# One small attention stage of a fused Perceiver block: GpSimd's order of work, the query products' place, and the engines that mask queries and add the residual

## The chip, the cores and the metric

The kernel runs on one core of a Trainium2 chip. The metric is the device time of one execution in microseconds (us), lower is better. TensorE (PE) multiplies matrices, VectorE (DVE), ScalarE (ACT) and GpSimd (POOL) do the elementwise work, SyncE (SP) issues DMAs.

## What is computed

The reference passes 64 sequences of 32 tokens with 256 features through six residual blocks in turn. The change is in the fifth, a causal attention of 16 heads of 16 features, with four groups of keys and values:

```
x = x + attn1(layernorm(x))

q  = einsum('bse,hed->bhsd', x, Wq) + bq[None, :, None, :]
kg = einsum('bse,ged->bgsd', x, Wk) + bk[None, :, None, :]
vg = einsum('bse,ged->bgsd', x, Wv) + bv[None, :, None, :]
k, v = repeat(kg, 4, axis=1), repeat(vg, 4, axis=1)
scores = where(causal, -inf, einsum('bhqd,bhkd->bhqk', q, k) / sqrt(16))
out = einsum('bhqk,bhkd->bhqd', softmax(scores), v)
```

After it comes the sixth block, a mixture of eight experts (`silu(x @ gate) * (x @ up)` times `down`, one expert a token), whose weights are 8 x 512 KB each for gate, up and down.

## The kernel before

The 2048 tokens are 16 tiles of 128 rows (`TILES`), and `x_sb` keeps all of them on chip. Each residual block is a stage of its own (`nc.Block`): every engine has its own list of instructions, semaphores order them between engines, and all engines meet at the end of a stage.

`small_attention` is used twice: with `cross=True` for the first block, with `cross=False` for the fifth, which this text calls the last small attention. Its names in the profile begin with `attn_` and lie between 939 and 1054 us. It is a software pipeline over the tiles. In step i an engine does its part for several tiles at once: in TensorE's list these are the scores of tile i (`scores`, product `ps_scores`), the transposes of the exponentials of tile i-1 (`turn_exps`, `ps_pT`), keys and values of tile i+1 (`keys_values`, `ps_kv`), its queries (`queries`, `ps_q`), the transposes of the normalised rows of tile i+2 (`turn`, `ps_T`), and the weighing of the values of tile i-1 (`weigh`, `ps_o`). The full steps run in a loop unrolled by two (`run_steps`).

For a tile the work passes through the engines so:

- GpSimd normalises the rows into `xn`, one buffer for all tiles, so that tile t waits for the transposes of tile t-1 (`turned`).
- TensorE transposes `xn`, ScalarE copies it to `xnT`, TensorE makes keys, values and queries.
- ScalarE adds the key bias (`kT`). VectorE adds the value bias (`v_rows`), and SyncE moves the values through DRAM into `v_blocks` (one DMA out, four DMAs in).
- VectorE adds the query bias and masks the queries once for each of four heads of a group, one instruction for each half of the features (`q_blocks`, L468).
- TensorE's scores begin with two products (L320) that write the causal mask into `ps_scores`, and wait for queries and keys before them.
- VectorE turns the scores (L506), takes the maximum (L511), subtracts it (L514); ScalarE takes the exponential; TensorE and ScalarE turn it; TensorE weighs the values; VectorE divides (L482, L486 into `outs`), adds to `x_sb` (L496), and takes the row's statistics for the next stage (L110).

Four things stand at the stage's ends. GpSimd first blanks `v_blocks` and `v_rows` (L259, L260), then issues 16 DMAs for the experts' up and down weights (L2187), and then begins to normalise. VectorE takes the last tile's mean and root (`moments.roots`, 12 links from L117 to L180) in step -1. At the end VectorE takes the roots of the other 15 tiles for the next stage before it divides tile 15. TensorE starts with one product that nobody reads (`keep_busy`, L278).

The order in time on VectorE is that of `step`: divide and residual of tile i-2, scores of tile i, values and queries of tile i+1.

## Time and profile before

| | |
|---|---|
| median of 3 runs | 1257.46 us (1254.38 to 1261.32) |
| the profiled execution | 1256.03 us |
| its span in the profile | 1254.2 us |
| busy over the span | PE 1141.8, DVE 720.3, ACT 443.3, POOL 267.3 us |
| last small attention | about 939 to 1054 us of the span |
| experts' first product | 1111.23 us in the chain of waits |

The span reaches from the first to the last instruction that the profile shows, and the 1.8 us between it and the execution's time lie around it. Times of instructions are counted from the start of the span. A row with x8 is eight like instructions together, and the number before the engine is the time from the first start to the last end.

### The profile page before, as it was taken

The page shows a single profiled execution, that of the slowest core. Times are in us where ns is not written, and L with a number is a line of the kernel's source. Part 1 is how long each engine was busy: PE and PEld are TensorE (multiplying, and loading weights), DVE is VectorE, ACT ScalarE, POOL GpSimd, SP SyncE. Part 2 cuts the span into 40 slices and gives each one's busy share as a digit, 9 for nine tenths or more (in the row PEclk, how much of TensorE's full clock was granted, in tenths as well). Part 3 has the DMA queues.
Part 4 walks back from the last instruction along what each step waited for, and adds up shares of the span by engine and source line. Part 5 has one row for each costly group of instructions (what it writes and reads, how often), then busy time and mean ns, then how long its engine had stood idle before and what let it go on. Part 6 is the DMA issues. An engine that isn't in the chain of part 4 may idle for free. (4 is left out here: it accounts for less than half of the span.)

```text
span 1254.2 us, 32458 instructions
## 1 busy us (share of the span) xinstructions
PE 1141.8 (91%) x12589; PEld 872.6 (70%) x12590; DVE 720.3 (57%) x1834; ACT 443.3 (35%) x1283; POOL 267.3 (21%) x343
## 2 busy tenths in 40 slices
PE   3899899999999889999969999999984887889997
PEld 1676688787887668987957777777754775546664
DVE  3788554455455465553257878888763998212221
ACT  0444353443343211211046555555521332112221
POOL 1600000000000000000144456445415220322222
PEclk9999899999999989999689999999996997899999
DMA  7521000000000076000002111111148112122221
GB/s 234 180 58 45 1 1 1 0 0 0 0 0 1 1 197 156 0 0 9 27 10 54 48 32 51 51 42 35 44 153 277 37 32 80 40 60 38 43 39 14
DMA packets 69644, 65.54 MB, mean 52 GB/s; under 512 B 32720, under 2 KB 60656, under 8 KB 68940
## 3 DMA queue, kind: packets, MB, share of 16 engines
q1 hardware_dynamic: 61612, 45.32, 14.0%
q0 software_dynamic: 7968, 19.32, 5.2%
q8 instruction: 45, 0.74, 0.2%
q14 instruction: 19, 0.16, 0.0%
HBM read 52.34 MB, written 13.19 MB: 52 GB/s over the span
## 5 line engine op out<-in xcount | busy, mean ns | idle before, releaser
L1532 ACT ACTIVATE xattn_exps<-xattn_ps_s,xattn_top 128x256 f32<-128x256 f32 x256 | 118.0, 475 | 77.5 <-DVE xattn_top L1600 77.5
L613 PEld LDWEIGHTS attn_ps_q<-attn_xnT,w_b_q 128*128 128x128 f32 x1024 | 118.8, 193 | 12.6 <-issue 12.6
L613 PE MATMUL attn_ps_q<-attn_xnT,w_b_q 128*128 128x128 f32 x1024 | 123.4, 276 | 0.0
L1099 POOL TENSOR_TENSOR fold_last_cos<-raw_last,all_consts 64x64 f32<-64x64 f32 x1 | 0.3, 314 | 538.3 <-POOLq L911 538.3
L667 PE MATMUL attn_ps_out<-w_b_o,attn_oT 128*128 128x256 f32 x480 | 106.5, 380 | 1.8 <-DVE all_x L848 1.5
L667 PEld LDWEIGHTS attn_ps_out<-w_b_o,attn_oT 128*128 128x128 f32 x480 | 90.0, 190 | 15.1 <-DVE all_x L848 2.4
L1607 DVE STREAM_TRANSPOSE xattn_expsT<-xattn_exps 128x1024 f32<-128x1024 f32 x64 | 79.5, 1242 | 22.6 <-ACT xattn_exps L1532 22.6
L721 ACT COPY attn_qT<-attn_ps_q 128x512 f32<-128x512 f32 x64 | 38.0, 594 | 148.2 <-PE attn_ps_q L613 148.2
L1597 DVE TENSOR_REDUCE xattn_raw_top<-xattn_ps_s 128x4 f32<-128x1024 f32 x64 | 77.8, 1216 | 13.6 <-PE xattn_ps_s L1424 13.3
L1424 PE MATMUL xattn_ps_s<-xattn_kT,xattn_qT 64*32 64x256 f32 x2048 | 69.6, 381 | 2.9 <-ACT xattn_exps L1532 2.9
L1434 PE MATMUL xattn_ps_o<-xattn_expsT,xattn_kv 32*64 32x256 f32 x2048 | 63.5, 380 | 4.6 <-DVE xattn_last_scores L1643 3.9
L799 DVE BATCH_NORM_STATS2 attn_out_stats<-attn_ps_out 128x6 f32<-128x256 f32 x15 | 6.5, 432 | 103.2 <-PE attn_ps_out L667 103.2
L1399 PEld LDWEIGHTS xattn_ps_o<-xattn_xnT,all_d_a 128*128 128x128 f32 x512 | 61.4, 197 | 6.2 <-issue 6.2
L1399 PE MATMUL xattn_ps_o<-xattn_xnT,all_d_a 128*128 128x128 f32 x512 | 65.5, 283 | 0.0
L942 PE MATMUL ffn_ps_h<-ffn_xnT,all_c 128*128 128x128 f32 x512 | 62.4, 281 | 0.0
L959 PE MATMUL ffn_ps_out<-all_c,ffn_masked 128*128 128x256 f32 x256 | 59.7, 380 | 1.6 <-DVE ffn_masked L1041 1.6
L1462 PE MATMUL xattn_ps_o<-all_d_b,xattn_ctxT 128*128 128x256 f32 x240 | 55.4, 384 | 6.1 <-POOL xattn_ctxT L1350 4.5
L1434 PEld LDWEIGHTS xattn_ps_o<-xattn_expsT,xattn_kv 32*64 32x64 f32 x2048 | 44.3, 131 | 23.4 <-issue 11.2
L942 PEld LDWEIGHTS ffn_ps_h<-ffn_xnT,all_c 128*128 128x128 f32 x512 | 59.8, 196 | 0.0
L1894 POOL DMA_INDIRECT out<-experts_y_out,experts_about x23 | 35.9, 1559 | 110.2 <-ACT experts_y_out L1966 108.5
L1976 DVE COPY experts_hT<-experts_ps_h 128x512 f32<-128x512 f32 x23 | 15.9, 692 | 68.4 <-PE experts_ps_h L1923 68.4
L1462 PEld LDWEIGHTS xattn_ps_o<-all_d_b,xattn_ctxT 128*128 128x128 f32 x240 | 44.4, 190 | 13.9 <-issue 6.2
(325 smaller groups left out, 2309.2 us busy)
## 6 DMA issues: line engine op xcount, KB each, us to landing
xattn_inverse<-xattn_inverse_rows SPq DMA_DIRECT2D x30, 256.0 KB, 4.1
all_c<-in_ctx SPq DMA_DIRECT2D x64, 64.0 KB, 1.9
moe_gate<-in_f_gate SPq DMA_DIRECT2D x8, 512.0 KB, 8.6
moe_up<-in_f_up POOLq DMA_DIRECT2D x8, 512.0 KB, 7.2
moe_down<-in_f_down POOLq DMA_DIRECT2D x8, 512.0 KB, 12.9
sorted_x<-all_zeros SPq DMA_DIRECT2D x1, 2944.0 KB, 15.7
experts_x_in<-sorted_x SPq DMA_DIRECT2D x23, 128.0 KB, 2.3
xattn_v_stage<-xattn_v_rows SPq DMA_DIRECT2D x16, 136.0 KB, 1.8
```

Of the source, the lines that this page charges most:

```text
L613: last = nc.tensor.matmul(ps_q[g % 2][:, h * P:(h + 1) * P], wq[:, c, head * DH:(head + 1) * DH], xnT[u][:, c, :], start=(c == 0), stop=(c ...
L667: last = nc.tensor.matmul(bank[:, 0:DIM], of_heads[:, h, :, :].rearrange("p b q -> p (b q)"), wo[:, h, :], start=(h == 0), stop=(h == HEAD ...
L721: nc.scalar.copy(qT[:, :, g, :].rearrange("p b (h q) -> p h b q", h=PER), ps_q[g % 2][:, :].rearrange("p (h b q) -> p h b q", h=PER, b=TB) ...
L942: last = nc.tensor.matmul(ps_h[half][:, j * P:(j + 1) * P], w1[:, c, f * P:(f + 1) * P], xnT[:, c, :], start=(c == 0), stop=(c == KC - 1))
L959: last = nc.tensor.matmul(ps_out[:, 0:DIM], masked[u][:, f, :], w2[:, f, :], start=(f == 0), stop=(f == chunks - 1))
L1399: last = nc.tensor.matmul(ps_q[part][:, n * P:(n + 1) * P], a_w[:, c, m * P:(m + 1) * P], xnT[:, c, :], start=(c == 0), stop=(c == KC - 1))
L1424: last = nc.tensor.matmul(ps_s[g % 2][SEQ * b:SEQ * b + SEQ, 512 * odd + nkeys * n:512 * odd + nkeys * (n + 1)], qT[u][rows, b, 2 * g + n, :],
L1434: nc.tensor.matmul(ps_o[b][64 * odd:64 * odd + 64, 0:DIM], kv[u][rows, j, :], expsT[u][rows, :, odd, :, j, :], start=(j == 0), stop=False, ...
L1462: last = nc.tensor.matmul(out_bank(t), ctxT[:, m, :, :].rearrange("p b s -> p (b s)"), b_w[:, m, :], start=(m == 0), stop=(m == pairs - 1))
L1532: nc.scalar.activation(exps[g % 2][:, nkeys * k:nkeys * (k + 1)], ps_s[g % 2][:, nkeys * k:nkeys * (k + 1)], ACT.Exp, bias=top[u][:, n:n + ...
L1597: nc.vector.tensor_reduce(of_group(raw_top), ps_s[g % 2][:, :].rearrange("p (o m n) -> p o m n", o=2, m=2), X_AXIS, ALU.max, negate=True). ...
L1607: nc.vector.transpose(expsT[u][:, g, :, :, :, :].rearrange("p o m j q -> p (o m j q)"), exps[g % 2][:, :])\
```

## The change

In the last small attention (`cross=False`):

- GpSimd normalises tile 0 before it blanks the buffers. Then it normalises tiles 1 to 15, with one of the 16 weight DMAs issued after each, and, from tile 5 on, the residual addition of the tile five before (`POOL_LEAD`) after that. The last five additions and the last DMA follow.
- TensorE makes the queries right after the scores, before the transposes of the exponentials. Their second half goes to a free part of `ps_T`'s bank, so that `turn` waits for ScalarE to have read it (`q1_ready`).
- VectorE masks the first half of the queries alone, and now ahead of the values. ScalarE masks the second half with four activations (scale is the mask, bias a table `q1_bias` that VectorE makes once, after the last tile's roots). ScalarE waits for this table before its first copy.
- VectorE no longer adds the residual. It waits for GpSimd's addition before it takes the statistics, and these now stand at the end of its step.
- VectorE takes the last tile's roots at the start of the stage.

In both uses of `small_attention` the first causal-mask product no longer waits for queries and keys. The core of the diff:

```diff
+POOL_LEAD = 5
...
+    ps_qm = [ps_q[:, 0:P], ps_q[:, P:2 * P]] if cross else [ps_q[:, 0:P], ps_T[:, DIM:DIM + P]]
...
         @block.gpsimd
         def _(pool):
+            def normalise(t):
+                if t == TILES - 1:
+                    pool.wait_ge(dve_roots, Moments.LAST_LINKS)
+                wait_count(pool, turned, t)
+                nc.gpsimd.tensor_scalar(xn[:, :], x_sb[:, t, :], moments.moments[:, t, 0:1], moments.factors[:, t:t + 1],
+                                        ALU.subtract, ALU.mult).then_inc(xn_ready, 1)
+
+            if not cross:
+                normalise(0)
             for u in range(2):
                 nc.gpsimd.memset(v_blocks[u][:, :, :, :, :], 0.0).then_inc(blank, 1)
                 nc.gpsimd.memset(v_rows[u][:, :, :, HD], 1.0).then_inc(blank, 1)
-            if beside:
+            if cross:
                 beside(pool)
...
+            else:
+                loads = beside(pool)
+                for t in range(1, TILES + POOL_LEAD):
+                    if t < TILES:
+                        normalise(t)
+                        next(loads)
+                    if t >= POOL_LEAD:
+                        pool.wait_ge(o_ready, t - POOL_LEAD + 1)
+                        nc.gpsimd.tensor_tensor(x_sb[:, t - POOL_LEAD, :], x_sb[:, t - POOL_LEAD, :],
+                                                outs[:, :, :].rearrange("p h d -> p (h d)"), ALU.add).then_inc(x_ready, 1)
+                next(loads)
...
             def turn(t):
                 pe.wait_ge(xn_ready, t + 1)
+                if not cross:
+                    wait_count(pe, q1_ready, t)
...
             def scores(t):
-                pe.wait_ge(q_ready, t + 1)
-                pe.wait_ge(k_ready, t + 1)
                 wait_count(pe, scores_out, t)
                 for p in range(2):
+                    if p == 1:
+                        pe.wait_ge(q_ready, t + 1)
+                        if not cross:
+                            pe.wait_ge(q1_ready, t + 1)
+                        pe.wait_ge(k_ready, t + 1)
                     nc.tensor.matmul(ps_scores[:, 512 * p:512 * p + 256], ident16, causal16, start=True, stop=False, skip_group_check=True)
...
                 if live(0):
                     scores(i)
+                if not cross and live(1):
+                    queries(i + 1, 1 - u)
...
+            if not cross:
+                act.wait_ge(bias_made, 1)
+
+            def queries_out(t):
+                act.wait_ge(q1_made, t + 1)
+                for r in range(PER):
+                    last = nc.scalar.activation(q_blocks[:, 1, r, :], ps_qm[1], ACT.Identity, bias=q1_bias[:, r:r + 1],
+                                                scale=consts[:, C_QMASK + r:C_QMASK + r + 1])
+                last.then_inc(q1_ready, 1)
...
+                moments.roots(dve, dve_roots, EPS_LN, 1.0, LAST, x_sb)
                 for s, n in loaded:
                     dve.wait_ge(s, n)
+                nc.vector.tensor_scalar(q1_bias[:, :], consts[:, C_QMASK:C_QMASK + PER], w["bq"][:, 1:2], None, ALU.mult).then_inc(bias_made, 1)
...
                 if live(-2):
                     outs_ready(i - 2)
-                    if not cross:
-                        residual(i - 2)
...
                 if live(1):
+                    queries_out(i + 1)
                     if not cross:
                         values_out(i + 1, 1 - u)
-                    queries_out(i + 1)
-                if live(-2) and cross:
+                if live(-2):
                     residual(i - 2)
```

GpSimd, the whole beginning of the last small attention, before. `moe_up` and `moe_down` are the experts' weights, `attn_xn` the normalised rows.

```order
L259 MEMSET attn_v_blocks 128x1088
L260 MEMSET attn_v_rows 128x4
L259 MEMSET attn_v_blocks 128x1088
L260 MEMSET attn_v_rows 128x4
L2187 DMA moe_up<-in_f_up 128x2x512 x8
L2187 DMA moe_down<-in_f_down 128x4x256 x8
L268 TENSOR_SCALAR attn_xn<-all_x,all_moments,all_moments_work 128x256 x16
```

GpSimd now: the start of the stage, and after "..." the part of one full step (tiles 6 and 1), where the addition into `all_x` stands third.

```order
L266 TENSOR_SCALAR attn_xn<-all_x,all_moments,all_moments_work 128x256
L272 MEMSET attn_v_blocks 128x1088
L273 MEMSET attn_v_rows 128x4
L272 MEMSET attn_v_blocks 128x1088
L273 MEMSET attn_v_rows 128x4
L266 TENSOR_SCALAR attn_xn<-all_x,all_moments,all_moments_work 128x256
L2224 DMA moe_up<-in_f_up 128x2x512
...
L266 TENSOR_SCALAR attn_xn<-all_x,all_moments,all_moments_work 128x256
L2224 DMA moe_up<-in_f_up 128x2x512
L284 TENSOR_TENSOR all_x<-all_x,attn_outs 128x256
```

Tile 0's normalising has moved from behind 16 DMAs and four memsets to the front, and a full step holds three instructions where it held one.

VectorE, one step of the loop of full steps, before.

```order
L482 RECIPROCAL attn_inverse<-attn_ps_o 128x16
L486 TENSOR_TENSOR attn_outs<-attn_ps_o,attn_inverse 128x256
L496 TENSOR_TENSOR all_x<-all_x,attn_outs 128x256
L109 MEMSET all_carrier 128x1
L110 BN_STATS all_row_stats<-all_x 128x6
L506 STREAM_TRANSPOSE attn_scores<-attn_ps_scores 128x256 x2
L511 TENSOR_REDUCE attn_top<-attn_scores 128x16
L514 TENSOR_TENSOR attn_shifted<-attn_scores,attn_top 128x512
L476 TENSOR_TENSOR attn_v_rows<-attn_ps_kv,all_e_bv 128x4x16
L468 SCALAR_TENSOR_TENSOR attn_q_blocks<-attn_ps_q,all_e_bq,all_consts 128x512 x2
```

VectorE, the same step now.

```order
L523 RECIPROCAL attn_inverse<-attn_ps_o 128x16
L526 TENSOR_TENSOR attn_outs<-attn_ps_o,attn_inverse 128x256
L542 STREAM_TRANSPOSE attn_scores<-attn_ps_scores 128x256 x2
L547 TENSOR_REDUCE attn_top<-attn_scores 128x16
L550 TENSOR_TENSOR attn_shifted<-attn_scores,attn_top 128x512
L509 SCALAR_TENSOR_TENSOR attn_q_blocks<-attn_ps_q,all_e_bq,all_consts 128x512
L517 TENSOR_TENSOR attn_v_rows<-attn_ps_kv,all_e_bv 128x4x16
L110 MEMSET all_carrier 128x1
L111 BN_STATS all_row_stats<-all_x 128x6
```

The addition is gone, one of two query instructions is gone, and the statistics of tile i-2 (L111, which reads what GpSimd adds) stand last, right ahead of the next step's reciprocal.

TensorE, one step of the loop, now. Its second half of the queries is written to `attn_ps_T`.

```order
L346 MATMUL attn_ps_scores<-all_causal,all_ident 128x256
L352 MATMUL attn_ps_scores<-attn_q_blocks,attn_kT 32x128 x16
L332 MATMUL attn_ps_q<-attn_xnT,all_e_q 128x128 x2
L332 MATMUL attn_ps_T<-attn_xnT,all_e_q 128x128 x2
L361 MATMUL attn_ps_pT<-all_consts,attn_exps 128x128 x4
L321 MATMUL attn_ps_kv<-attn_xnT,all_e_k 128x128 x4
L324 MATMUL attn_ps_kv<-all_e_v,attn_xnT 128x64 x2
L306 MATMUL attn_ps_T<-all_consts,attn_xn 128x128 x2
L372 MATMUL attn_ps_o<-attn_v_blocks,attn_expsT 32x68 x16
```

Before, the four query products (L311) stood between the values and the transposes of `attn_xn`; the number of products is the same.

## Rows read from the trace of the kernel before

**Rows 1.** The page, busy time of the engines.

```profile
PE 1141.8 (91%) x12589; PEld 872.6 (70%) x12590; DVE 720.3 (57%) x1834; ACT 443.3 (35%) x1283; POOL 267.3 (21%) x343
```

**Rows 2.** Timeline, start of the stage: start us, us, engine, line.

```profile
939.15 1.00 POOL L259 MEMSET attn_v_blocks<- 128x1088 f32 x1 [16.35 <-POOLq L1301]
941.11 5.80 POOL L2187 DMA_DIRECT2D moe_up<-in_f_up  x8
952.92 1.24 POOL L268 TENSOR_SCALAR attn_xn<-all_x,all_moments,all_moments_work 128x256 f32<-128x256 f32 x1
954.30 0.66 PE L287 MATMUL attn_ps_T<-all_consts,attn_xn 128*128 128x128 f32 x2 [14.02 <-POOL attn_xn L268]
```

**Rows 3.** Busy by stretch: PE, PEld, DVE, ACT, POOL, then PEclk, DMA share, GB/s.

```profile
939.00:954.00 15.00, 1.10 (x2) 0.30 (x2) 0.00 (x0) 0.20 (x1) 14.80 (x21) 0.70 0.75 265
954.00:960.00 6.00, 5.17 (x23) 4.80 (x24) 0.23 (x1) 1.00 (x3) 1.37 (x2) 0.50 1.03 355
985.00:1040.00 55.00, 47.82 (x951) 40.22 (x932) 51.61 (x124) 21.59 (x51) 11.01 (x9) 1.00 0.17 33
```

**Rows 4.** Timeline of VectorE: the last tile's roots, and what follows.

```profile
961.49 0.42 DVE L117 BATCH_NORM_STATS2 all_row_stats<-all_x 128x6 f32<-128x256 f32 x1
964.32 0.78 DVE L506 STREAM_TRANSPOSE attn_scores<-attn_ps_scores 128x256 f32<-128x256 f32 x2
```

**Rows 5.** Timeline of TensorE: the score products of tiles 2 and 15.

```profile
973.85 0.67 PE L326 MATMUL attn_ps_scores<-attn_q_blocks,attn_kT 64*32 64x128 f32 x32
1043.47 0.67 PE L326 MATMUL attn_ps_scores<-attn_q_blocks,attn_kT 64*32 64x128 f32 x32
```

**Rows 6.** Timeline of VectorE, one full step.

```profile
985.91 0.76 DVE L506 STREAM_TRANSPOSE attn_scores<-attn_ps_scores 128x256 f32<-128x256 f32 x2
988.04 0.22 DVE L476 TENSOR_TENSOR attn_v_rows<-attn_ps_kv,all_e_bv 128x64 f32<-128x64 f32 x1
988.17 1.40 DVE L468 SCALAR_TENSOR_TENSOR attn_q_blocks<-attn_ps_q,all_e_bq,all_consts 128x512 f32<-128x512 f32 x2
989.49 0.25 DVE L482 RECIPROCAL attn_inverse<-attn_ps_o 128x16 f32<-128x16 f32 x1
989.77 0.42 DVE L486 TENSOR_TENSOR attn_outs<-attn_ps_o,attn_inverse 128x256 f32<-128x256 f32 x1
990.34 0.42 DVE L496 TENSOR_TENSOR all_x<-all_x,attn_outs 128x256 f32 x1
990.91 0.43 DVE L110 BATCH_NORM_STATS2 all_row_stats<-all_x  x1
```

**Rows 7.** Timeline of the same step: TensorE and GpSimd.

```profile
989.63 0.39 PE L320 MATMUL attn_ps_scores<-all_causal,all_ident 128*128 128x256 bf16 x2 [0.74 <-DVE attn_q_blocks L468]
989.95 0.67 PE L326 MATMUL attn_ps_scores<-attn_q_blocks,attn_kT 64*32 64x128 f32 x32
990.55 0.66 PE L335 MATMUL attn_ps_pT<-all_consts,attn_exps 128*128 128x128 f32 x4
991.04 1.06 PE L302 MATMUL attn_ps_kv<-attn_xnT,all_e_k 128*128 128x128 f32 x8
993.28 0.38 PE L287 MATMUL attn_ps_T<-all_consts,attn_xn 128*128 128x128 f32 x2
993.76 1.22 POOL L268 TENSOR_SCALAR attn_xn<-all_x,all_moments,all_moments_work 128x256 f32<-128x256 f32 x1 [4.16 <-PE attn_ps_T L287]
```

**Rows 8.** Groups of GpSimd and ScalarE: count, busy us, mean ns, idle before.

```profile
L1254 POOL TENSOR_TENSOR all_c<-all_c 128x256 f32<-128x256 f32 x64 | 44.7, 731 | 7.0 <-PE xattn_ps_o L1388 4.8 <-POOL all_c L1247 1.9
L406 ACT ACTIVATE attn_kT<-attn_ps_kv,all_e_bk 128x128 f32<-128x128 f32 x32 | 10.0, 364 | 17.6 <-PE attn_ps_kv L305 17.6
```

**Rows 9.** By line, first small attention: ns min/median/max, first and last start.

```profile
L2115 POOL TENSOR_SCALAR w_b_q<-w_b_q,w_b_g x16: 914/916/1248, 35.3 to 50.1; 128x256 f32<-128x256 f32 x16
L514 DVE TENSOR_TENSOR xattn_shifted<-xattn_scores,xattn_top x16: 691/692/853, 37.2 to 119.4; 128x512 f32<-128x512 f32 x16
```

**Rows 10.** Waits of the SyncE queue, 938 to 1060 us: total, times, longest.

```profile
SPq L253 <- DMA attn_v_stage<-attn_v_rows: 19.0, 16, 5.8
```

52 lines of the change are left out of this document (23 added, 29 removed).

## The prediction

> **What bounds the kernel now.** I read the page first: no engine is busy for the whole span, but TensorE comes near (1141.8 of 1254.2 us) [rows 1], so a gain has to come from a stretch in which it waits or runs at its low clock. The busy times by stretch and the timeline of the changed stage show two such places. The first is its start. The stage begins at 939.15, and TensorE's first transposes at 954.30, after 14.02 us idle until GpSimd's normalised rows: GpSimd spent four memsets and 16 DMA issues first [rows 2]. In those 15 us TensorE is busy 1.10 us, and when work comes its granted clock is 0.50, the 1.2 GHz level [rows 3]. VectorE adds a delay: it takes the last tile's roots from 961.49 to 964.32, and only then turns tile 0's scores [rows 4].
>
> The second place is the steady part. Score products lie at 973.85 (tile 2) and 1043.47 (tile 15) [rows 5]: 69.62 / 13 = 5.355 us a tile. There VectorE is busy 51.61 of 55 us, the rest being gaps of hand-over, TensorE 47.82 at full clock [rows 3]; VectorE's instructions follow one another [rows 6], and TensorE waits 0.74 us a tile for the masked queries [rows 7]. So VectorE bounds the steady part. ScalarE has room (21.59 of 55). After the stage everything hangs on its end, so I let what it saves go through to the end.
>
> **The start.** GpSimd's first normalising moves from 952.92 to 939.15, 1.24 us long [rows 2]: transposes from 940.5 instead of 954.30, 13.8 us earlier. ScalarE's copy would follow at 941.0, but now waits for the query bias, behind VectorE's roots: 964.32 - 961.49 = 2.83 us from 939.2, so about 942.1, a small table included, 1.1 us of the 13.8 lost.
>
> From there I step through three tiles, with TensorE's durations at full clock, because it now pauses only about 2 us at a time. It takes 2.24 us for keys, values and queries (993.28 - 991.04) and 0.60 for scores (990.55 - 989.95) [rows 7]. I split the 2.24 as 0.95 for the four query products and 1.29 for the six of keys and values, an estimate by their number and width. ScalarE's copy about 0.36, as its nearest form [rows 8]: `xnT` at 942.5, queries to 943.5, keys and values to 944.9. ScalarE masks from 943.7; four activations at 0.364 each, the mean of the nearest form [rows 8], less overlaps, make 1.3, and two for the keys 0.63: 945.7. Scores of tile 0 about 945.9. Tile 1: 0.60 + 0.95, then 1.3 + 0.63 on ScalarE and hand-overs, 4.0 in all: 949.9. Tile 2: TensorE's whole list, 0.60 + 0.95 + 0.49 + 1.29, 0.3 for two transposes (four take 0.49), causal mask 0.32, and for the weighing the 0.65 that is left of its 4.6 a tile, plus 0.3 of waiting, 4.9: 954.8. Before it was 973.85: the start gives **19.0 us**, 13.8 from the order on GpSimd, the rest from the clock, the roots' place and the halved query work, less the bias wait. The GpSimd blanks (four memsets) are done by 942.4, before SyncE needs them.
>
> **The steady part.** VectorE loses half of 1.40 us and the addition, 0.42 with a hand-over that takes it to 0.57 (990.91 - 990.34) [rows 6]: 5.355 - 0.70 - 0.5 = 4.15 us. TensorE alone needs 5.355 less its 0.74 wait, about 4.65 to 4.75. Were that all, a tile would take 4.75. But the addition now stands on GpSimd behind the normalising of tile i+3 and a DMA issue, the first of which waits for TensorE's transposes of tile i+2, and VectorE may not start the next step before. This closes a loop through two tiles, which I add up from the start of VectorE's transposes of tile i:
>
> - to the end of the halved queries of tile i+1: 988.04 - 985.91 = 2.13, plus 0.70 [rows 6]: 2.83
> - to the score products: hand-over 0.06 (989.57 to 989.63) and the second causal product 0.16: 0.22 [rows 7]
> - scores 0.60, exponentials' transposes 0.49, queries, keys and values 2.24: 3.33 to the transposes of tile i+3 [rows 7]
> - to GpSimd 0.48 (993.28 to 993.76) [rows 7]
> - normalising 1.22 [rows 7], DMA issue 5.80 / 8 = 0.73 [rows 2], addition 0.73, from an addition of the same shape elsewhere [rows 8]: 2.68
> - back on VectorE: hand-over and memset 0.13, statistics 0.43, reciprocal 0.28, division 0.43 [rows 6]: 1.27.
>
> That is 10.81 us for two tiles, **5.40 a tile** against 5.355. So halving VectorE's work gains nothing in the steady part: the bound goes over to the loop GpSimd - VectorE - TensorE. Over 13 tiles it costs 13 x 0.045 = 0.6 us, which tile 3, still at TensorE's pace, gives back. TensorE goes on waiting about 0.7 us a tile on average, alternately nothing and 1.3. ScalarE gets 1.3 us a tile; the transposes that wait for it start 1.78 us after the queries, so 0.4 us hides it. If it took 0.5 us more, the loop would grow by about 0.15 a tile, 2 us.
>
> **What costs nothing.** The DMAs for the experts were all issued by 952.92 [rows 2]; now the last one is issued at the stage's end, but the experts begin 57 us after it. SyncE's queue waits for each value store 19.0 / 16 = 1.2 us on average [rows 10] and has more than 3 us of slack a tile. In the first small attention VectorE has its work ready for the scores without TensorE waiting, so the earlier causal product changes nothing.
>
> **The end.** The last residual was VectorE's at 0.42. Now it is GpSimd's 0.73 with a hand-over 0.07, and the last DMA issue 0.73 behind it: 1.1 us more. Tile 14's statistics wait for GpSimd too, before the roots: 0.4. Together 1.5 us lost.
>
> **A collision.** In the first small attention GpSimd multiplies weights while VectorE subtracts the maximum (two inputs from on-chip memory). Three such subtractions fall on it: one took 853 instead of 692 ns, one of GpSimd's took 1248 instead of 916, so a meeting cost (0.16 + 0.33) / 3 = 0.16 us on average [rows 9]. Before, the changed stage has no such meeting; now there are one or two in each round of two tiles, of subtraction with normalising. I take 1.0 us over the stage, with 0 and 2.2 (0.33 in each of 6.5 rounds) as ends from these rows.
>
> The Trainium skill is harsher ("SBUF — State Buffer", Who interferes with whom): a VectorE instruction with two SBUF inputs and a GpSimd instruction that reads SBUF exclude each other for a whole instruction. The rows agree that they touch, not that one fully waits. By that rule the sum would be 3 us larger, the rival "full exclusion" below.
>
> **The sum.** 19.0 - 1.5 - 1.0 = 16.5 us less. From the profiled execution's own 1256.03: 1239.5. It lies 1.4 under the median of the runs; both are within the runs' scatter, and I forecast **1239.5**.
>
> **Rivals.**
> - *The loop is shorter* (0.15). If GpSimd's three instructions overlap, so that the DMA issue does not hold up the addition, or hand-overs are shorter, the tile falls to TensorE's 4.75: 13 x 0.65 = 8.4 more, 1231. For it: the issue is work of a queue, and the addition needs nothing from it. Against: eight issues in a row took 0.73 each, and normalising came only after all 16 [rows 2].
> - *Full exclusion* (0.17). In the loop one of two subtractions starts within a normalising and would wait for its end, about 0.6 us a round: 6.5 x 0.6 = 3.9 instead of 1.0, so 1242.5. For it: 1248 ns once. Against: the two other meetings cost 0.16 and nothing.
> - *Low clock at the start* (0.08). TensorE gets 1.2 GHz, as it did at 954 [rows 3], until about 950: the three tiles take 4 us longer, 1243.5. Against: it was idle 14 us then, and has no pause above 2 us now.
> - *Slower: the values come too late* (0.05). SyncE stores each tile's values and reads them back; now a 512 KB load is under way beside each. With 16 loads under way one such store took 5.8 us to land [rows 10]. Were it so for every tile, a tile would take 5.8 plus the issues of five DMAs, some 2 us: 7.8, and 13 x 2.45 = 32 less 17 gained is 15 us slower, 1272. It decides from 5.355 + 17 / 13 = 6.7 us a tile on. Against: that was behind a queue of 16, and one load is a sixteenth of it.
> - *It does nothing* (0.05): between 1251 and 1264, if the loop takes 6.4 to 7 us a tile, through some of the same, or what follows the stage waits for a DMA now issued later.
>
> The forecast case has the remaining 0.50, with 1236 to 1243 as its own range (bounds of the collision, ScalarE's 2 us, half a microsecond on each of the start's three tiles). The range over the cases, 1231 to 1247, leaves out the two last rivals and some of the tails. A difference of 0.5% (6.3 us) is about what a measurement of this kernel can tell from no change. Faster: 0.50 + 0.15 + 0.17 + 0.08, and a little of the last case: 0.90; same 0.04; slower 0.06.
>
> **What the changed profile would show.** Transposes of tile 0 at 940.5 and a full clock in the first 15 us; score products of tile 2 at 954.8. Score products 5.4 us apart on average, in pairs of about 4.8 and 6.0. VectorE idle over 1 us a tile, before the statistics, until GpSimd's addition; GpSimd's three instructions in a row, 2.7 us together. ScalarE's four masks in 1.3 us. An even 4.75 would show my loop wrong; an addition over 1 us, subtractions over 0.9, or TensorE waiting for `v_blocks`, would show the rivals. The prediction fails if the loop's terms are off by more than 1.2 us a round, or if the start isn't carried through to the experts.

## The result, and the profile after

The changed kernel takes 1253.93 us (median of 20 runs) against 1261.55 for the kernel before in runs on the same chips (median of 20): a ratio of 0.9936, with a 95% interval of 0.9922 to 0.9951. It is faster by 0.6%, about 8 us, where I had forecast 16.5. 19 of the 20 runs lie between 1247.72 and 1257.79, all above 1247, the top of my range; one run of each kernel was far longer (2890.98 and 1947.75 us) and is left out of the ratio. The profiled execution took 1249.35 us, with a span of 1247.1.

The page's first row, against [rows 1]: ScalarE and GpSimd gained work, VectorE lost some.

```profile
PE 1144.8 (92%) x12589; PEld 875.7 (70%) x12590; DVE 704.9 (57%) x1803; ACT 463.3 (37%) x1347; POOL 279.7 (22%) x359
```

**The start.** The timeline of the stage's first microseconds (start, duration, engine, line; against [rows 2]):

```profile
938.76 1.23 POOL L266 TENSOR_SCALAR attn_xn<-all_x,all_moments,all_moments_work 128x256 f32<-128x256 f32 x1 [16.42 <-POOLq L1333]
...
940.13 0.41 PE L306 MATMUL attn_ps_T<-all_consts,attn_xn 128*128 128x128 f32 x2 [0.30 <-POOL attn_xn L266]
...
942.07 0.37 ACT L424 COPY attn_xnT<-attn_ps_T 128x256 f32<-128x256 f32 x1 [3.15 <-DVE attn_q_bias L499]
...
943.49 1.72 PE L321 MATMUL attn_ps_kv<-attn_xnT,all_e_k 128*128 128x128 f32 x8
...
943.69 1.50 ACT L466 ACTIVATE attn_q_blocks<-attn_ps_T,attn_q_bias,all_consts 128x128 f32<-128x128 f32 x4 [1.25 <-PE attn_ps_T L332]
...
947.06 0.67 PE L352 MATMUL attn_ps_scores<-attn_q_blocks,attn_kT 64*32 64x128 f32 x32
...
956.08 0.67 PE L352 MATMUL attn_ps_scores<-attn_q_blocks,attn_kT 64*32 64x128 f32 x32
```

The score product of tile 0 starts 8.30 us after the stage, that of tile 2 17.32 us after it; before it was 34.70 [rows 2, 5]. That is 17.4 us won of the 19.0 forecast. ScalarE's first copy waits for VectorE's bias until 942.07, as worked out; what I had not counted is that the keys, 1.06 us elsewhere, take 1.72. The busy times by stretch say why (PE, PEld, DVE, ACT, POOL, PEclk, DMA share, GB/s): behind a pause of 1.95 us the granted clock goes to 0.50, the 1.2 GHz level, for some three microseconds.

```profile
942.00:944.00 2.00, 1.51 (x12) 1.51 (x13) 0.75 (x1) 0.68 (x2) 1.88 (x2) 0.93 0.00 0
944.00:946.00 2.00, 2.00 (x12) 2.00 (x12) 0.01 (x1) 1.20 (x5) 0.00 (x0) 0.50 0.61 193
946.00:948.00 2.00, 1.83 (x39) 0.96 (x38) 0.37 (x2) 0.88 (x3) 1.50 (x2) 0.72 0.25 87
```

The same pause did not always have this effect. In two of the experiments below, e11_early_dma and e17_add_front, TensorE paused for the same 1.95 us, the clock stayed at 1.00, and tile 0's score product started 7.3 us after the stage instead of 8.30. The stretch of e11_early_dma with tile 0's keys:

```profile
950.00:952.00 2.00, 2.00 (x19) 2.00 (x19) 0.75 (x1) 0.87 (x3) 1.32 (x2) 1.00 0.00 0
```

**The steady part.** The score product of tile 15 starts at 1028.74, so tiles 2 to 15 take 72.66 us, 5.59 a tile, where it was 5.355 [rows 5] and I had 5.40. From tile 5 to tile 14 the steps alternate, 5.99 and 5.37. The timeline of the forecast round, from one VectorE transposing to that of two tiles later:

```profile
986.69 0.77 DVE L542 STREAM_TRANSPOSE attn_scores<-attn_ps_scores 128x256 f32<-128x256 f32 x2
...
988.83 0.74 DVE L509 SCALAR_TENSOR_TENSOR attn_q_blocks<-attn_ps_q,all_e_bq,all_consts 128x512 f32<-128x512 f32 x1
...
989.84 0.67 PE L352 MATMUL attn_ps_scores<-attn_q_blocks,attn_kT 64*32 64x128 f32 x32
...
993.28 0.41 PE L306 MATMUL attn_ps_T<-all_consts,attn_xn 128*128 128x128 f32 x2
...
993.60 0.69 DVE L550 TENSOR_TENSOR attn_shifted<-attn_scores,attn_top 128x512 f32<-128x512 f32 x1
...
993.80 1.58 POOL L266 TENSOR_SCALAR attn_xn<-all_x,all_moments,all_moments_work 128x256 f32<-128x256 f32 x1 [3.24 <-PE attn_ps_T L306]
...
995.34 0.80 POOL L2224 DMA_DIRECT2D moe_down<-in_f_down  x1
...
996.17 0.73 POOL L284 TENSOR_TENSOR all_x<-all_x,attn_outs 128x256 f32<-128x256 f32 x1
...
996.97 0.06 DVE L110 MEMSET all_carrier<- 128x1 f32 x1 [1.89 <-POOL all_x L284]
...
998.04 0.77 DVE L542 STREAM_TRANSPOSE attn_scores<-attn_ps_scores 128x256 f32<-128x256 f32 x2
```

The loop is there in the order I wrote it down: 2.88 + 0.27 + 3.44 + 0.52 + 3.10 + 1.14 = 11.35 us, against 2.83 + 0.22 + 3.33 + 0.48 + 2.68 + 1.27 = 10.81. The largest part of the difference is GpSimd's: the normalising takes 1.58 instead of 1.22, because it starts under a running subtraction (993.60), and the issue of a `moe_down` DMA 0.80 instead of 0.73. The other row of tiles, the even beside the odd, has no such meeting, and 11.37 us too, for another reason:

```profile
987.82 1.22 POOL L266 TENSOR_SCALAR attn_xn<-all_x,all_moments,all_moments_work 128x256 f32<-128x256 f32 x1 [2.28 <-PE attn_ps_T L306]
...
988.22 0.69 DVE L550 TENSOR_TENSOR attn_shifted<-attn_scores,attn_top 128x512 f32<-128x512 f32 x1
...
989.82 0.75 POOL L284 TENSOR_TENSOR all_x<-all_x,attn_outs 128x256 f32<-128x256 f32 x1
...
990.63 0.06 DVE L110 MEMSET all_carrier<- 128x1 f32 x1 [0.93 <-POOL all_x L284]
...
990.86 0.43 DVE L111 BATCH_NORM_STATS2 all_row_stats<-all_x  x1 [0.17 <-issue]
...
992.08 0.77 DVE L542 STREAM_TRANSPOSE attn_scores<-attn_ps_scores 128x256 f32<-128x256 f32 x2
```

Here VectorE returns from the addition's end (990.57) to its transposes in 1.51 us instead of 1.14; one row shows it idle for 0.17 with nothing to wait for ("issue"). Its steps stand in a loop of two tiles. That this is where the loop turns is a reading here; e13_unrolled below tests it.

**The end.** The timeline:

```profile
1038.76 0.72 POOL L284 TENSOR_TENSOR all_x<-all_x,attn_outs 128x256 f32<-128x256 f32 x1 [5.27 <-DVE attn_outs L526]
1039.42 0.78 POOL L2224 DMA_DIRECT2D moe_down<-in_f_down  x1
...
1045.50 0.41 SPq L1763 DMA_DIRECT2D out<-all_x  x1
1045.53 0.14 POOL L1880 IOTA moe_tokens_tokens<- 128x16 int32 x1 [5.33 <-POOLq L2025]
...
1045.70 1.19 PE L1787 MATMUL route_ps_unread<-all_consts 128*128 128x512 f32 x1 [8.27 <-PEq L2025]
```

After the last addition the stage stands still for 6.02 us, though the experts need that DMA only 59 us later. TensorE is idle for 8.27. In the kernel before it was 1.33 (timeline):

```profile
1053.07 0.42 DVE L496 TENSOR_TENSOR all_x<-all_x,attn_outs 128x256 f32<-128x256 f32 x1
1054.82 0.41 SPq L1731 DMA_DIRECT2D out<-all_x  x1
```

The view of the weight DMAs' line has the sixteen land after 4.2 to 5.2 us. For the last one alone (1030 to 1046 us) it says:

```profile
DMA to landing us min/median/max: 4.3/4.3/4.3
```

So the last DMA lands at 1043.7, and the next stage's first instruction follows 1.8 us later. The same 1.8 us, to 0.02, lie between this landing and the next stage in all seven traces that end with a weight DMA and nothing longer (changed, e2, e3, e4, e5, e13 and e14 in the table below), while their gaps range from 5.95 to 6.14. What the stage's end follows is the landing.

All the traces side by side, one execution of each kernel, in us. "To tile 2" is from the stage's first GpSimd instruction to the score product of tile 2, "tiles 2-15" between score products, "tail" from that of tile 15 to the end of the last addition, "gap" from there to the next stage's first instruction, "next" from there to the experts' first product. The sum leaves "next" out. Ratios are to the kernel before, from runs on the same chip, and are not the quotient of two medians in this table; e1 to e19 had their own runs of the kernel before (medians 1260.04 to 1261.79).

| kernel | to tile 2 | tiles 2-15 | tail | gap | sum | next | median, us | ratio (95%) |
|---|---|---|---|---|---|---|---|---|
| before | 34.70 | 69.62 | 10.02 | 1.33 | 115.7 | 56.4 | 1261.55 | |
| changed | 17.32 | 72.66 | 10.74 | 6.02 | 106.7 | 58.6 | 1253.93 | 0.9936 (0.9922-0.9951) |
| e8_start_only | 21.16 | 69.62 | 10.03 | 1.32 | 102.1 | 59.0 | 1248.14 | 0.9912 (0.9884-0.9940) |
| e1_last_dma | 17.56 | 74.70 | 10.74 | 2.50 | 105.5 | 58.8 | 1251.38 | 0.9911 (0.9882-0.9940) |
| e11_early_dma | 16.31 | 75.63 | 10.75 | 2.49 | 105.2 | 56.4 | 1250.98 | 0.9920 (0.9891-0.9948) |
| e6_warm | 17.32 | 72.71 | 10.76 | 12.92 | 113.7 | 58.1 | 1255.50 | 0.9950 (0.9924-0.9976) |
| e5_top_psum | 18.46 | 71.61 | 10.75 | 6.04 | 106.9 | 58.8 | 1253.03 | 0.9927 (0.9896-0.9957) |
| e13_unrolled | 17.77 | 72.35 | 10.75 | 6.05 | 106.9 | 56.4 | one, 1255.92 | |
| e14_both | 17.84 | 70.12 | 10.75 | 6.13 | 104.8 | 58.7 | one, 1247.92 | |
| e4_add_first | 17.41 | 68.66 | 10.75 | 6.13 | 103.0 | 58.8 | 1249.99 | 0.9895 (0.9842-0.9949) |
| e3_lead4 | 17.82 | 70.12 | 10.75 | 6.14 | 104.8 | 58.9 | 1245.68 | 0.9864 (0.9805-0.9922) |
| e2_add_dve | 17.39 | 63.03 | 10.52 | 5.95 | 96.9 | 56.3 | 1245.17 | 0.9897 (0.9817-0.9978) |
| e12_best | 16.09 | 72.14 | 10.98 | 1.35 | 100.6 | 58.8 | 1243.20 | 0.9842 (0.9800-0.9883) |
| e15_best_unr | 16.14 | 73.12 | 10.52 | 1.37 | 101.2 | 56.2 | 1244.18 | 0.9878 (0.9847-0.9909) |
| e16_front | 22.28 | 72.82 | 10.52 | 1.35 | 107.0 | 59.0 | 1251.62 | 0.9923 (0.9894-0.9952) |
| e17_add_front | 25.07 | 75.27 | 10.74 | 2.50 | 113.6 | 58.7 | 1259.22 | 0.9994 (0.9967-1.0022) |
| e18_two_last | 14.94 | 66.46 | 10.51 | 1.36 | 93.3 | 59.2 | 1240.47 | 0.9839 (0.9808-0.9871) |
| e19_staged_first | 15.88 | 70.66 | 12.51 | 1.36 | 100.4 | 59.2 | 1244.67 | 0.9876 (0.9847-0.9906) |

The stage became 115.67 - 106.74 = 8.9 us shorter, which agrees with the ratio (0.64% of 1261.55 is 8.1). The two profiled spans differ by 7.1: the changed stage began 0.4 us earlier, and the next one took 2.2 us longer. Its starts scatter too, from 938.8 to 947.9 us over the executions, from what lies ahead of it; the sums inside the stage are steadier than a single time. e6_warm differs from the changed kernel only behind the last tile and so repeats it: 17.32 and 72.71. Not every kernel is so steady. e2_add_dve's four executions reach from 1236.14 to 1255.15 us, and its trace is of the shortest; e12_best's six reach from 1233.96 to 1252.57, and its trace is of the second longest (1250.14).

### The profile page after: what moved, and what is told of

The parts are those of the page before. It is cut to its first block and busy times, and to the rows that moved or that the text cites. A ratio compares the mean times of both kernels' runs of the same rounds, so it can differ in the third digit from the quotient of the medians.

```text
span 1247.1 us, 32531 instructions
## 1 busy us (share of the span) xinstructions
PE 1144.8 (92%) x12589; PEld 875.7 (70%) x12590; DVE 704.9 (57%) x1803; ACT 463.3 (37%) x1347; POOL 279.7 (22%) x359
```

## The experiments

### The start alone

e8_start_only is the kernel before with GpSimd's new order alone:

```
+                normalise(0)
             for u in range(2):
                 nc.gpsimd.memset(v_blocks...); nc.gpsimd.memset(v_rows...)
+                loads = beside(pool)
+                for t in range(1, TILES):
+                    normalise(t)
+                    next(loads)
+                next(loads)
```

> The kernel before with one part of the change alone: GpSimd scales tile 0 ahead of the blanking and issues one weight DMA a tile, the last behind its last normalising; query products, masks and the addition stay where they were. Theory 1 (nearly all of the gain is the start): the score product of tile 0 starts 9 to 11 us after the stage's start instead of 23.0, that of tile 2 19 to 21 instead of 34.7; tiles 2 to 15 take 69.6 us as before; the stage's end waits little, since the last DMA is issued some 10 us ahead of it, so the gap is 1.3 to 2 us; the time is 12 to 14 us below the kernel before. Rival (the order of GpSimd alone moves the wait elsewhere in the start, since TensorE's keys and queries then set it): less than 8 us.

Tile 2 at 21.2, the same 69.62 for the tiles after it, a gap of 1.32, 13.5 us less in the stage; tile 0, at 6.6, came sooner than the 9 to 11 expected. This part alone brings more than the whole change (102.1 against 106.7): what else the change does costs 4.6 us. That is read from the traces; the two ratios, 0.9912 and 0.9936, lie the same way, but their intervals overlap.

### The end

e1_last_dma issues the sixteenth DMA behind the fifteenth, e11_early_dma behind tile 2's normalising; neither has one behind the last addition.

```
                     next(loads)
+                    if t == 2:            # e1: t == TILES - 1
+                        next(loads)
...
-            next(loads)                   # behind the last addition
```

> The changed kernel, with the last weight DMA issued right behind the fifteenth (after tile 15's normalising) and none behind the last addition. Theory (the stage's end waits for that DMA to land, and TensorE's long pause there costs it clock in the next stage): the gap from the end of the last addition to the next stage's first instruction falls from 6.0 to about 1.3 us, and the next stage, up to the experts' first product, from 58.6 to about 56.4 us; span 1247.1 - 4.7 - 2.2 = 1240. Rival (the gap is a cost of having GpSimd work at a stage's end, whatever it is): gap and span stay within 1 us. Second rival (the longer next stage has nothing to do with the pause): gap 1.3, next stage still 58.6, span 1242.4.

> The changed kernel with one alteration: GpSimd issues two weight DMAs behind its normalising of tile 2, early in the stage, and none behind the last addition. Theory 1 (the stage's end waits for the landing of the DMA that GpSimd issued last): the gap between the last addition and the next stage's first instruction falls from 6.0 to about 1.3 us, as before the change, and the stage's loop stays at 72 to 73 us for tiles 2 to 15; the time falls by 4 to 5 us. Rival (the gap is the block's own end, whatever was issued): the gap stays at 6 us and the time is that of the changed kernel.

The gap fell from 6.02 to 2.50 and 2.49, not to 1.3. The timeline of e11_early_dma shows what is left:

```profile
1048.17 0.72 POOL L286 TENSOR_TENSOR all_x<-all_x,attn_outs 128x256 f32<-128x256 f32 x1 [5.26 <-DVE attn_outs L527]
...
1051.38 0.41 SPq L1764 DMA_DIRECT2D out<-all_x  x1
```

So the DMA issued last costs 3.5 us, and an addition that stands last on GpSimd another 1.2, since every kernel with VectorE's addition and no late DMA has a gap of 1.32 to 1.37. The two do not simply add: with the DMA last, e2_add_dve has a gap of 5.95 with VectorE's addition too, so there the DMA alone costs 4.6.

Neither kernel kept what it won: tiles 2 to 15 took 74.7 and 75.6 us. In both, behind pauses of TensorE of 1.4 us or more, the granted clock fell to 0.50 for some three microseconds: once in e1_last_dma, at 1030, behind the two issues at tile 15, and twice in e11_early_dma, at 1003 and 1016. A stretch of e11_early_dma:

```profile
1004.00:1006.00 2.00, 2.00 (x16) 2.00 (x10) 1.93 (x5) 0.00 (x0) 0.00 (x0) 0.50 0.59 218
```

The changed kernel has no such fall between tiles 2 and 15. Two issues in a row thus cost more than the 0.8 us that the second one takes, though how two issues at tile 2 lead to a pause seven tiles on, the traces don't show.

e6_warm puts 16 unread products behind TensorE's list.

```
-            nc.tensor.matmul(ps_kv[:, 0:512], ident, consts[:, 0:512], ...)
+            for n in range(1 if cross else 16):
+                nc.tensor.matmul(ps_kv[:, 0:512], ident, consts[:, 0:512], ...)
```

> The changed kernel with one alteration: behind the last product of TensorE's list in the stage stand 16 products whose results nobody reads (some 15 us of work while TensorE waits for the stage's end) instead of 1. Theory 1 (the next stage starts at the low clock, since TensorE stood still for 8.3 us ahead of it, and this costs it 2.2 us): the granted clock of the next stage's first 4 us is 1.0 instead of 0.50, the next stage (to the experts' first product) falls from 58.6 to about 56.4 us, and the gap stays at 6.0. Rival (the clock there is set otherwise, or what the next stage waits for is not TensorE's): it stays at 58 to 59 us.

The products outlasted the wait, and the gap became 12.9. The next stage did begin at full clock, which fell to 0.50 after some seven microseconds, and it took 58.1 us: a warm start is no remedy. With the column "next" the theory falls altogether: 56.2 to 56.4 us in five kernels and 58.1 to 59.2 in thirteen, at gaps of 1.3 and of 6 alike. The 2.2 us in the profiled pair are no effect that I can tie to the change; what decides between the two lengths stays open.

### The round of two tiles

e5_top_psum lets the subtraction read its maximum from PSUM; e13_unrolled writes VectorE's steps out; e14_both does both.

```
+    if not cross:                         # e5, e14
+        top = ps_scores[:, 768:768 + HEADS]
...
-            run_steps(dve, step, -2, TILES + 1, 2, TILES - 3)
+            for i in range(-2, TILES + 2):    # e13, e14, not in the cross attention
+                step(i, i % 2, lambda d: 0 <= i + d < TILES)
```

> The changed kernel with one alteration: VectorE's maximum (16 numbers a row) is written to PSUM instead of SBUF, so the subtraction that follows reads one operand from SBUF and one from PSUM. Theory 1 (GpSimd's normalising is held by the subtraction because that reads two SBUF operands): the normalising is 1.22 us in all tiles, two tiles' round loses about 0.35 us, tiles 2 to 15 take about 70 instead of 72.7 us, 2 to 3 us less in all. Rival (GpSimd and VectorE collide whenever both touch SBUF): every second normalising still takes 1.5 us or more, and tiles 2 to 15 stay at 72 to 73 us.

> The changed kernel with one alteration: VectorE's steps of this stage are written out instead of standing in a loop of two steps. Its trace shows two rows of tiles that hardly share anything, the even and the odd ones, both with 11.35 us a round: in one the normalising is held by the subtraction (1.5 to 1.6 us instead of 1.22), in the other VectorE comes back 0.36 us later from GpSimd's addition to its transposes (1.51 instead of 1.14), behind its statistics, where its loop turns. Theory 1 (each of the two delays alone holds the round): without the turn the return is 1.1 us in all tiles, but the collision keeps the round at 11.3 us and tiles 2 to 15 at 72 to 73 us. Rival (the late return has nothing to do with the loop's turn): every second return stays at 1.4 to 1.5 us.

> The changed kernel with both alterations: the maximum in PSUM, and VectorE's steps written out. Theory 1 (collision and turn each hold one of the two rows of tiles): only both together shorten the round, to 11.0 us (11.35 less 0.36), and tiles 2 to 15 take 69 to 70 us, against 71.6 with the maximum in PSUM alone and 72.7 in the changed kernel. Rival (something else holds the round, such as GpSimd's three instructions against TensorE): 71 to 72.7 us.

With the maximum in PSUM all normalisings took 1.22 us, as theory 1 said of the collision, but the rounds stayed at 11.36, held by the late return: of the 2 to 3 us for tiles 2 to 15 there came 1.05, and the start was longer by as much (its clock stayed at 0.50 for seven microseconds). With the steps written out (e13_unrolled) the return is 1.0 us in every tile, against 1.15 and 1.51, and since this moved the meeting away at first, the round became what I had added up, 990.75 - 979.94 = 10.81. So theory 1, by which the collision alone would keep it at 11.3, did not hold there. The timeline:

```profile
979.94 1.23 POOL L266 TENSOR_SCALAR attn_xn<-all_x,all_moments,all_moments_work 128x256 f32<-128x256 f32 x1 [3.29 <-PE attn_ps_T L306]
...
990.75 1.22 POOL L266 TENSOR_SCALAR attn_xn<-all_x,all_moments,all_moments_work 128x256 f32<-128x256 f32 x1 [3.30 <-PE attn_ps_T L306]
...
995.77 1.22 POOL L266 TENSOR_SCALAR attn_xn<-all_x,all_moments,all_moments_work 128x256 f32<-128x256 f32 x1 [2.26 <-PE attn_ps_T L306]
...
996.03 0.83 DVE L550 TENSOR_TENSOR attn_shifted<-attn_scores,attn_top 128x512 f32<-128x512 f32 x1
...
1006.98 1.75 POOL L266 TENSOR_SCALAR attn_xn<-all_x,all_moments,all_moments_work 128x256 f32<-128x256 f32 x1 [2.47 <-PE attn_ps_T L306]
...
1007.02 0.69 DVE L550 TENSOR_TENSOR attn_shifted<-attn_scores,attn_top 128x512 f32<-128x512 f32 x1
...
1008.42 0.68 PE L372 MATMUL attn_ps_o<-attn_v_blocks,attn_expsT 128*32 128x68 f32 x32 [1.56 <-DMA attn_v_blocks<-attn_v_stage]
```

Then the steps went to 6.6, 6.1 and 6.05. Three things lie together there: TensorE waited 1.56 us for the values (1008.42), the granted clock behind it was 0.50 for some three microseconds, and one normalising took 1.75. The step of 6.6 is 5.05 and TensorE's wait. e14_both has no collision and no late return: 10.8 to 11.3 us a round, 70.1 us for the tiles, where theory 1 had 69 to 70, though from 1005 us on TensorE waits 0.5 to 0.9 us a tile for the values. It is the one run of these that shortens the stage, by 2; both e13 and e14 were run once.

These rows also show how the two engines hold each other, and that it goes both ways. A subtraction that starts 0.26 us into a normalising takes 0.83 instead of 0.69 (996.03); e4_add_first has one at 0.25 with 0.84, and the changed kernel 0.74 at 0.35 and 0.69 to 0.71 from 0.38 on. VectorE's addition, in e2_add_dve, takes 0.67 instead of 0.42 when it starts 0.15 us in. In each case the delay ends 0.40 us after the normalising's start. In the other direction the normalising pays what is left of the subtraction, less 0.12: 0.46 of 0.58, 0.36 of 0.48, 0.27 of 0.40 in the changed kernel. Where both start together, within 0.06 us, it is the normalising that waits (1.72 to 1.75).

e4_add_first turns addition and DMA issue round, e3_lead4 sets GpSimd's lead to 4, e2_add_dve puts the addition back on VectorE behind the division (GpSimd's list then has normalisings and DMAs alone, and its last DMA waits for tile 15's division).

```
-    next(loads)                           # e4: behind the addition instead
-POOL_LEAD = 5
+POOL_LEAD = 4                             # e3
...
+                else:                     # e2, in residual(t)
+                    dve.wait_ge(o_ready, t + 1)
+                    nc.vector.tensor_tensor(row(x_sb, t), row(x_sb, t), outs..., ALU.add)
```

> The changed kernel with GpSimd's order in a step changed to normalise, add, DMA issue: the issue (0.80 us) leaves the loop, all else stays. Theory: the two-tile loop falls by 0.8, from 11.36 to 10.6, 5.3 a tile; tiles 2 to 15 from 72.7 to 67.7, span about 1242. If the issue held nothing up: no difference. If the loop is not what bounds: none either, or less than 2 us.

> The changed kernel with POOL_LEAD = 4: GpSimd adds a tile's residual one step earlier in its list, so that VectorE's statistics of a tile no longer wait for the normalising and the DMA issue of the same step. Theory (the loop through two tiles is what bounds): 4.8 to 4.9 us a tile, tiles 2 to 15 in 63 instead of 72.7 us, VectorE's waits for GpSimd nearly gone, span about 1247 - 10 = 1237. Rival (GpSimd now waits for VectorE's division with the next normalising queued behind it, and the bound moves there): 5.3 us a tile or more, span 1243 or more.

> The changed kernel with the residual addition back on VectorE, at the place in its step where it now waits for GpSimd; GpSimd only normalises and issues DMAs. Theory (a loop GpSimd - VectorE - TensorE of 11.36 us for two tiles sets the steady part): the loop is gone, score products come every 4.8 us instead of 5.68, so tiles 2 to 15 take about 62.5 instead of 72.7 us; the end's 6 us gap stays. Span about 1247 - 10 = 1237. Rival (TensorE or ScalarE sets the pace, ScalarE's four masks take 1.5 us): still 5.4 to 5.7 a tile, span 1246 to 1248.

e4 gave 5.28 a tile: the issue of 0.8 us does stand in the loop. e2 gave 4.85, TensorE's own pace: the addition's place on GpSimd is what closes the loop. e3 gave 70.1 us for the tiles, 5.39 a tile, with no collision in it. That is the rival's number (5.3 or more), but the rival's wait is only a part of it: between 965 and 1020 us GpSimd waited 2.3 us for VectorE's division, in three steps, while TensorE waited 6.6 us, up to 1.3 a tile, for the blanked values, a wait that the changed kernel does not have. Which of the two held the tiles, no run shows.

### The values and the weights

e12_best is e2_add_dve with e11's early DMA, and with ScalarE's bias wait moved from its start to its first mask; e15_best_unr has VectorE's steps written out as well.

```
-            if not cross:
-                act.wait_ge(bias_made, 1)
             def queries_out(t):
+                if isinstance(t, int) and t == 0:
+                    act.wait_ge(bias_made, 1)
```

> The changed kernel with what the runs so far speak for: the addition back on VectorE, behind the division (63.0 us for tiles 2 to 15), two weight DMAs behind tile 2's normalising so that none is issued at the end, and ScalarE waiting for the scaled bias only ahead of its first mask. Theory 1 (with a DMA as the last thing on GpSimd the end waits some 3.5 us for its landing, with GpSimd's addition 1.2 us more for GpSimd): the gap is 1.3 us, tiles 2 to 15 take 63 to 64, the start is 0 to 1.1 us shorter, and the time is 20 to 23 us below the kernel before (ratio 0.982 to 0.985). Rival (a DMA fewer at the end costs the same at tile 2, or the gap is not the DMA's): 15 to 18 us below.

> The kernel above (addition on VectorE, no DMA at the end, later wait for the bias) with VectorE's steps written out as well. Theory 1: VectorE's return at the loop's turn is 0.26 us late in every second step there, but TensorE sets the pace (4.8 to 4.9 us a tile), so at most 0.1 us a tile, 1 us in all. Rival (VectorE sets the pace): 0.13 us a tile, 1.7 us or more. A loss is possible if VectorE's longer list costs something where it is fetched.

The gap is 1.35 and the bias wait gone: tile 0's score product starts 5.93 us after the stage in all five kernels without it, against 7.3 to 9.4 in the eleven with it. But the tiles took 72.1 us, not 63, in the traced execution; the ratio of 0.9842 over all of them lies inside what I expected. e15_best_unr gained nothing on it (73.1 us for the tiles, and two intervals that overlap). The view of waits of e12_best, 965 to 1020 us (total, times, longest), names the reason:

```profile
POOL attn_xn L266 <- PE attn_ps_T L302: 36.1, 10, 4.1
ACT attn_q_blocks L462 <- PE attn_ps_T L328: 21.2, 9, 3.0
PEld attn_ps_o L368 <- DMA attn_v_blocks<-attn_v_stage: 10.4, 10, 1.6
PE attn_ps_o L368 <- DMA attn_v_blocks<-attn_v_stage: 8.0, 10, 1.4
```

and its timelines of GpSimd and SyncE show what lies behind it: the weight DMA goes out at 984.26, the store of the values at 985.35, the four that read it back at 989.09, once it has landed.

```profile
984.26 0.81 POOL L2224 DMA_DIRECT2D moe_down<-in_f_down  x1
...
985.35 0.38 SPq L253 DMA_DIRECT2D attn_v_stage<-attn_v_rows  x1
...
989.09 1.74 SPq L257 DMA_DIRECT2D attn_v_blocks<-attn_v_stage  x4
...
990.93 0.38 SPq L253 DMA_DIRECT2D attn_v_stage<-attn_v_rows  x1
```

In the steady part of e18_two_last the store stands ahead of the weight DMA:

```profile
989.79 0.34 SPq L253 DMA_DIRECT2D attn_v_stage<-attn_v_rows  x1
...
991.27 0.79 POOL L2224 DMA_DIRECT2D moe_down<-in_f_down  x1
...
991.70 1.94 SPq L257 DMA_DIRECT2D attn_v_blocks<-attn_v_stage  x4
```

Four kernels varied this. e16_front (VectorE's addition) and e17_add_front (GpSimd's) issue four weight DMAs behind each of tiles 1 to 4; e18_two_last is e12_best with the pair at tile 15; e19_staged_first adds a wait.

```
+                    if t <= 4:                # e16, e17
+                        for n in range(4):
+                            next(loads)
...
+                    wait_count(pool, v_staged, 16 * (t - 1))   # e19, ahead of next(loads)
+                    if t == TILES - 1:        # e18, e19
+                        next(loads)
```

> The kernel with the addition on VectorE and the later bias wait, but the 16 weight DMAs issued four at a time behind the normalising of tiles 1 to 4, none later. Its sibling with one a tile took 72.1 us for tiles 2 to 15, and there TensorE waited for the blanked values: the small DMA that stages them was issued 0.2 to 1.1 us behind a weight DMA and landed after 3.7 us (median), against 2.3 in the run that took 63.0 us and 1.5 in the kernel before, where no weight DMA was under way. Theory 1 (the staging DMA queues behind the weights, and once it is late SyncE issues the next one late too, right behind the next weight DMA, so that the state keeps itself up): with no weight DMA from tile 6 on, the staging lands in 1.5 to 2 us, the last ten tiles take 4.8 us each or less, and the time is 1233 to 1240 us. The first tiles may lose up to 3 us. Rival (the values are late by SyncE's own serial work, a landing and five issues a tile): the last tiles stay at 5.3 to 5.8 us.

> The changed kernel (addition on GpSimd) with the 16 weight DMAs issued four at a time behind the normalising of tiles 1 to 4, none later, and none at the end. Theory 1 (from tile 5 on, GpSimd has 0.80 us less a tile, and no weight DMA delays the values): the two-tile round falls from 11.35 by 0.80 to about 10.5, so the last ten tiles take 5.3 us each, the gap is 2.5 us as with the last DMA issued early, and the time is 1245 to 1249 us. Rival (the DMA's issue does not hold the round, or TensorE does at 4.8): 4.8 or 5.7 us a tile.

> The kernel with the addition on VectorE and the later bias wait, one weight DMA a tile, and the sixteenth right behind the fifteenth (tile 15) instead of two behind tile 2. Theory 1 (two weight DMAs at tile 2 pushed the staging DMA of the values into the state where it is always issued just behind a weight DMA and lands after 3.7 us; without them it keeps to 2.3): tiles 2 to 15 take 63 to 65 us instead of 72.1, the gap is 1.3, the time 1233 to 1240 us. Rival (the state comes by chance of small shifts, whatever tile 2 does): 72 us in some executions, 63 in others, and the times scatter from 1233 to 1252 as they did.

> The kernel above, and GpSimd issues the weight DMA of a tile only once the staging DMA of the values that were made at the same time has landed. Theory 1 (the weight DMA that is under way when the staging DMA is issued is what makes the values late): in no execution can a weight DMA be issued just ahead of a staging DMA, so the staging lands in 1.5 to 2.5 us, tiles 2 to 15 take 62 to 64 us, TensorE waits for no values, and the times are 1232 to 1238 us with less scatter. Rival (the weight DMA then holds the four DMAs of blanked values that follow the staging, which land after 3 to 4 us instead of 2, and the tiles stay at 5.3 us or more).

The median time from a store's issue to its landing, the last column of the view of DMAs: first of the kernel before, then of e12_best, then of e16_front.

```profile
attn_v_stage<-attn_v_rows SPq DMA_DIRECT2D x16, 34.0 KB, 1.5
```
```profile
attn_v_stage<-attn_v_rows SPq DMA_DIRECT2D x16, 34.0 KB, 3.7
```
```profile
attn_v_stage<-attn_v_rows SPq DMA_DIRECT2D x16, 34.0 KB, 1.5
```

e16 confirms theory 1 in the part free of weights: 4.8 to 4.9 a tile. It pays for it earlier than I allowed, and with 1251.6 us misses the 1233 to 1240 by far: tiles 2 and 3 took 12.2 and 12.8 us with four loads under way each. e17 gave 5.15 and 5.52 in turn, 10.67 a round, against 10.5 expected, again after steps of 13.6 and 10.1; at 1259.2 us nothing is left of the change's gain. e18 fell into the late order (a store just behind a weight DMA) at tiles 3 and 4 (6.9 and 6.3 us) and came out by itself, to 4.8 to 4.9: the pair at tile 2 is not what leads there, but without it the traced execution did get out. With 66.5 us for the tiles (63 to 65 expected) and the shortest stage it is, with e12_best, the fastest kernel here: 1240.47 us, ratio 0.9839, 1.0% below the changed kernel. e19 was to forbid the late order, and did the opposite: the store that it waits for was itself issued only 1.6 us behind the weight DMA before it, landed after 3.5 us, and now held GpSimd's next normalising as well, 3.2 to 3.4 us each. That a weight DMA just ahead of a store goes with its late landing holds in all these traces; what inside the DMA path delays it, none shows, and my placing of the wait was wrong.

## Why the prediction was wrong, step by step

- **The bound and its shift: right.** VectorE's halved work gains nothing in the steady part, the loop GpSimd - VectorE - TensorE takes over, in pairs of about 4.8 and 6.0 at first (4.80 and 6.16, tiles 3 and 4).
- **The start: right in kind, the gain forecast 1.6 us too large.** From tile 0 to tile 2 I had 8.9 us, and it took 9.02. The loss lies ahead of tile 0's score product: 8.30 instead of 6.75 us. The bias wait costs 8.30 - 5.93 = 2.4, not 1.1: 1.4 for the copy (3.3 us after the stage's start, 1.9 in e18_two_last) and 1.0 for the clock, which stays at 1.00 without the pause. So my rival "low clock at the start" (0.08), which I argued away with pauses of no more than 2 us, came true for 1.0 of its 4 us, behind a pause of 1.95; in e11 and e17 it did not come. The masks took 457 ns each against 364 from the nearest form, 1.50 us in all.
- **The steady part: two terms mis-sized, 2.0 us.** Collision and loop together were to cost 1.0 us and cost 3.0 (72.66 - 69.62). The "back on VectorE" term was one number, while every second tile has the turn of VectorE's loop in it; and the collision was priced by an average of three meetings in another place, 0.16, when it costs the normalising 0.3 to 0.5 whenever that starts second. In the changed kernel each of the two holds one row of tiles at 11.35. Without the collision the rounds stayed there (e5); without the turn they fell to my sum of 10.81 at first, as the engines then met otherwise (e13); without both the stage became 2 us shorter (e14). TensorE's own pace, which I put at 4.65 to 4.75 us a tile, is 4.81 to 4.90 in e2 and e16: the rival "the loop is shorter" would have been worth some 7 us, not 8.4.
- **"What costs nothing", the last DMA: the step that failed, and the largest.** I wrote that the last DMA is issued at the stage's end but the experts begin 57 us after it, and gave it 0.73 us of issue. I had looked for who reads its data, and the stage's end waits for it without reading. With GpSimd's addition, end and gap cost 0.7 + 4.7 = 5.4 us instead of 1.5: 0.7 for the slower addition, 3.5 for the landing and 1.2 for GpSimd, in the order in which e1 takes them away. That is 3.9 of the 7.5 us that I was off in the stage (1.6 + 2.0 + 3.9). I had the possibility in one clause of a rival with 0.05, "what follows the stage waits for a DMA now issued later", and never looked at what ends a stage.
- **Full exclusion: the wrong half of it.** The case that I priced, a subtraction that starts under a running normalising and waits for its end, costs next to nothing here: 0.69 (988.22, above), since it starts 0.4 us in. The case that costs is the other one. A normalising that starts under a subtraction takes 1.49 to 1.68 instead of 1.22, and at 993.80 some 0.49 of the subtraction were left: here about 0.36 of it was paid. The Trainium skill ("SBUF — State Buffer", Who interferes with whom) has the two shut each other out for a whole instruction. The traces agree with its cause in e5_top_psum, where one SBUF input fewer ended it. They agree with the length on VectorE's side, to 0.12 us, but not on GpSimd's, where only the first 0.40 of the normalising's 1.22 us hold VectorE. The measurement decides.
- **The values come too late: not in this kernel, but in several of my variants.** No wait of TensorE for them stands in the steady part of the changed kernel, though the store's median landing is 2.6 us instead of 1.5. At 3.7, in e12, they set the pace.
- **"Everything hangs on its end": right.** The gain inside the stage (8.9 us) and the gain in the times (8.1) agree within a microsecond.

## What to carry to other kernels

When a DMA is moved, ask not only who reads its data but which stage's end stands behind its queue: issue the last one well ahead (the kernels here that did had it out 17 us or more before the last addition's end, and it lands after 4 to 6). A slack engine that is given a short instruction becomes part of a loop if the busy engine waits for it in every step; add the loop up for each parity of an unrolled loop, with the turn and the collisions in it, before calling the work hidden. A pause of two microseconds on TensorE can cost more than itself by the clock behind it, so look at the granted clock behind each pause that an edit adds. Test the parts of a change alone: here one of them brings 13.5 us and the rest together gives back 4.6.
